# Four score tiles of each head group maximised over an fp16 copy made by ScalarE, with a new attention order and three reordered norm stages

## The chip, the cores and the metric

The kernel runs on one core of one Trainium2 chip. The metric is the device time in microseconds. Engines are TensorE (PE in the profile), its weight loads (PEld), VectorE (DVE), ScalarE (ACT), GpSimd (POOL) and SyncE, which issues the DMAs (SPq).

## The reference

Two layers over 1024 tokens of width 512, each half of a layer followed by a residual and a layer norm:

```python
x = layernorm(x + selective_scan(x))          # 16 states, softplus dt
x = layernorm(x + (silu(x @ Wg.T) * (x @ Wu.T)) @ Wd.T)          # 1792 wide
x = layernorm(x + attention(x))               # 32 heads of 16, rope, causal softmax, wo
x = layernorm(x + ffn(x))                     # 1376 wide, 4-bit GPTQ weights
```

The softmax of head n and token t is over `scores[n, t, s] / 4` for s <= t. Any number near the row's maximum may be subtracted before the exponential; the kernel searches that maximum first.

## The kernel before

Everything lies in one SBUF arena; each engine has one hand-written program, and semaphores order them.

*Scan* (to 201 us): 64 scans of VectorE (line 1354), products by GpSimd, sums by TensorE. *First norm*: `turn_first`, `first_stats`, `first_shift`, `first_normalise`, `turn_normed`, and `first_high` and `first_rest`, which split a normalised tile into two fp16 parts; `xl_done` counts tiles whose remainder is there. *First FFN* (213 to 363 us): 28 units `gate_up0(n)` (line 603), each of half the tokens, 16 gate and 16 up matmuls of 512 columns. `unit0_slot` gives unit n its two PSUM banks: units 0 to 3 alternate between two slots, unit 4 has the slot of unit 2 and waits for its Silu (`silu_done`). Then `down0` and the projections of q, k and v tile by tile (line 710), with rope on VectorE, the split by ScalarE and GpSimd, and the transposes `turn_stack`.

*Attention.* Heads go in NG = 8 groups of four (two pairs r, and two row halves b = 0, 1 of the array, 64 rows each). Search units (`search`, line 694; `max_units`): the scores of one query tile i against up to 512 keys, query on the PSUM rows, of one head, or of two heads where the columns are few: 40 units a group, 12 for the first four tiles (half 0) and 28 for the others (half 1). The last key tile of a row gets a mask added by two small matmuls (line 706). VectorE reduces each unit to its negated maximum (`maxima`, line 1563). `negate` (line 1581) joins the two key ranges of half 1, `turn_maxima` (line 733) transposes the maxima to rows, `keep_rows` (line 1587) copies them, and `put_rows` on SyncE sends them into q_st, where they are an additional row of the queries. So `keys` (line 743) gives scores with the maximum already subtracted, in the layout key by query; ScalarE takes the exponential (line 1114), GpSimd zeroes the corner of diagonal tiles (line 1254), `values` (line 757) multiplies with v and a column of ones, using the whole array in four column tiles. `keep_out` (line 1100), `turn_out` and `divide` finish a half of a group.

Search units, turns and outputs share a ring of three PSUM banks (`ring_slot`, line 684): unit n waits until unit n - 3 is read (`ring_read`). Keys have two pairs of banks, values one bank. The order of all steps, the same for all engines, is `ORDER`: the letters of `PATTERN` (s search, k keys, v values, n negate, t turn, o out) are gone through once for each group, and `START` says at which step of its own sequence each letter begins. 24 of group 0's search units (tiles below 6) are done early, during the projections (`early_units`, at most two at each of three places in a tile's projections), in a ring of two banks in which unit n waits for n - 1 reads.

*Second norm* (664 to 702 us): `second_out` (the wo projection), `second_stats`, `second_shift`, `second_root`, `second_normalise`, `second_turn`, `second_high`, `second_low`; then `gate_up1` of the second FFN, which wants four remainders (`xl_done`) for its first half of tokens and all eight for the second. *Second FFN* to 811 us, unpacking the 4-bit weights on VectorE, GpSimd and ScalarE beside it, and `down1` with the last norm (`norm_stage(3, ..., turn=False)`), each tile written out as it is done.

## Time and profile before

| | us |
|---|---|
| median of 3 runs | 879.1 (876.25 to 879.51) |
| profiled execution | 876.1 |
| its span | 874.4 |
| TensorE busy | 804.1 (92%) |
| VectorE busy | 642.1 (73%) |
| ScalarE busy | 443.5 (51%) |
| GpSimd busy | 301.8 (35%) |

The span is from the first to the last instruction. A busy share is that of the whole span, over stages with different limits. A matmul's row reaches to its modelled end, so rows of matmuls that follow each other overlap, and TensorE can read as busy where its array isn't full. A row of the order of time joins neighbours of one kind (xN), and "[... <-X]" is idle time before it and what ended it.

### The profile page before, as it was taken

How to read it: one execution, taken by the hardware profiler on the slowest of the kernel's cores; microseconds unless marked ns; L12 is line 12 of the kernel's file. 1: busy time of each engine (PE TensorE's matmuls, PEld its weight loads, DVE VectorE, ACT ScalarE, POOL GpSimd, SP SyncE). 2: the span in 40 equal slices, each digit the busy share in tenths (PEclk: the TensorE clock that was granted, in tenths of full speed). 3: DMA queues.
4: the chain of work that ended last, by engine and by line, in shares of the span. 5: the costliest groups of instructions: out<-in, count | busy, mean ns of one | idle time of the engine just before them, and what ended most of it. 6: DMA issues, size and time to landing. Idle time of an engine off the chain costs nothing.

```text
span 874.4 us, 19489 instructions
## 1 busy us (share of the span) xinstructions
PE 804.1 (92%) x8137; PEld 383.5 (44%) x8137; DVE 642.1 (73%) x900; ACT 443.5 (51%) x584; POOL 301.8 (35%) x217
## 2 busy tenths in 40 slices
PE   7669787787999999999989999999989999999997
PEld 2434344444444444455544444444424444444443
DVE  4999999997565333444669999999976677775344
ACT  4976666546654321254427777777786433332100
POOL 0699899991001000155421222121143222221000
PEclk9589999999999999999988999999999999999999
DMA  6900000005230000000000000000132013330001
GB/s 215 365 3 3 3 3 2 3 4 168 97 115 1 1 0 1 1 1 1 1 1 2 2 2 2 2 2 3 37 115 86 1 59 118 123 110 0 13 36 48
DMA packets 20017, 38.25 MB, mean 44 GB/s; under 512 B 5009, under 2 KB 10961, under 8 KB 19938
## 3 DMA queue, kind: packets, MB, share of 16 engines
q1 hardware_dynamic: 19938, 37.10, 12.4%
q8 instruction: 61, 1.00, 0.5%
q14 instruction: 18, 0.15, 0.1%
HBM read 34.87 MB, written 2.16 MB: 42 GB/s over the span
## 4 chain that ended last, share of the span: by engine, by line
PE 76%; DVE 13%; issue 4%; POOL 3%; ACT 2%; DMA 1%; SPq 1%; DVEq 0%; ACTq 0%; POOLq 0%
PE ps L832 13%; PE ps L613 11%; PE ps L590 10%; PE ps L769 8%; DVE arena L1354 7%; PE ps L702 7%; PE ps L867 7%; PE ps L666 6%; PE ps L753 3%; PE ps L706 3%; POOL arena L1205 2%; PE ps L679 2%; PE ps L509 2%; PE ps L465 1%; PE ps L778 1%
## 5 line engine op out<-in xcount | busy, mean ns | idle before, releaser
L1563 DVE TENSOR_REDUCE arena<-ps 128x1 f16<-128x512 f32 (+3 forms) x320 | 181.4, 630 | 6.4 <-PE ps L706 4.1
L1114 ACT ACTIVATE arena<-ps 128x1024 f32<-128x1024 f32 (+2 forms) x160 | 143.4, 940 | 60.6 <-PE ps L753 58.8
L1205 POOL TENSOR_TENSOR arena<-arena 128x1024 f32<-128x1024 f32 x62 | 152.0, 2485 | 9.3 <-DVE arena L1354 8.9
L1354 DVE TENSOR_TENSOR_SCAN arena<-arena,ps 128x1024 f32<-128x1024 f32 x64 | 142.1, 2269 | 2.0 <-PE ps L509 1.7
L832 PE MATMUL ps<-arena 128*128 128x512 f16 x528 | 114.5, 379 | 1.4 <-DVE arena L1671 1.4
L702 PE MATMUL ps<-arena 64*128 64x512 f16 (+3 forms) x384 | 99.6, 339 | 0.7
L1254 POOL TENSOR_SCALAR_AFFINE_SELECT arena<-arena 128x512 f32<-128x512 f32 x64 | 43.4, 685 | 162.4 <-ACT arena L1114 162.3
L613 PE MATMUL ps<-arena 128*128 128x512 f16 x448 | 97.5, 379 | 1.5 <-DVE arena L1494 1.5
L957 ACT ACTIVATE arena<-arena,negA 128x1024 f32<-128x1024 f32 x64 | 72.8, 1146 | 45.4 <-DVE arena L1354 43.2
L509 PE MATMUL ps<-arena 64*128 64x64 f16 x3072 | 60.0, 196 | 35.1 <-DVE arena L1354 31.8
L509 PEld LDWEIGHTS ps<-arena 64*128 64x128 f16 x3072 | 52.2, 98 | 86.3 <-DVE arena L1354 75.0
L590 PE MATMUL ps<-arena 128*128 128x512 f16 x384 | 86.6, 379 | 1.6 <-DVE arena L1453 1.6
L769 PE MATMUL ps<-arena 128*32 128x512 f32 (+3 forms) x768 | 80.2, 497 | 0.3 <-POOL arena L1254 0.3
L832 PEld LDWEIGHTS ps<-arena 128*128 128x128 f16 x528 | 51.6, 98 | 63.3 <-DVE arena L1671 1.6
L465 PE MATMUL ps<-arena,ident_sb 64*64 64x512 f32 x512 | 71.5, 634 | 2.0 <-POOL arena L1205 1.2
L753 PE MATMUL ps<-arena 64*128 64x512 f16 (+3 forms) x384 | 70.3, 328 | 2.4 <-ACT arena L1114 2.2
L613 PEld LDWEIGHTS ps<-arena 128*128 128x128 f16 x448 | 43.7, 98 | 53.6 <-issue 1.7
L702 PEld LDWEIGHTS ps<-arena 64*128 64x128 f16 x384 | 30.8, 94 | 69.0 <-DVE arena L1563 49.6
L867 PE MATMUL ps<-arena 128*128 128x512 f16 x264 | 57.1, 379 | 0.0
L706 PE MATMUL ps<-mask_b,picks_b 64*128 64x128 bf16 x512 | 55.9, 221 | 0.0
L590 PEld LDWEIGHTS ps<-arena 128*128 128x128 f16 x384 | 36.4, 98 | 43.7 <-DVE arena L1453 1.8
L666 PE MATMUL ps<-arena 128*128 128x512 f16 x224 | 49.3, 379 | 0.0
(173 smaller groups left out, 973.1 us busy)
## 6 DMA issues: line engine op xcount, KB each, us to landing
arena<-in_w_q_dram SPq DMA_DIRECT2D x11, 768.0 KB, 4.2
arena<-c_rows SPq DMA_DIRECT2D x16, 512.0 KB, 10.7
arena<-in_w_s_dram SPq DMA_DIRECT2D x11, 384.0 KB, 4.9
arena<-in_x_fm_dram SPq DMA_DIRECT2D x8, 256.0 KB, 4.3
out_dram<-arena SPq DMA_DIRECT2D x8, 256.0 KB, 2.0
arena<-in_wg_dram SPq DMA_DIRECT2D x1, 1792.0 KB, 10.2
arena<-in_wu_dram SPq DMA_DIRECT2D x1, 1792.0 KB, 7.3
arena<-in_wd_dram SPq DMA_DIRECT2D x1, 1792.0 KB, 11.3
```

The costliest lines, as they stand in the source:

```text
L509: last = nc.tensor.matmul(ps[:, 2 * (i % 2) + r, q * SUB:(q + 1) * SUB], dtx_tok[c % 2][rows, s, q, :], diag[n][rows, e, q, :], start=(k = ...
L590: last = nc.tensor.matmul(banks(bank, 1), part[:, c, ds(t * P, P)], wsp[:, w, s, c, :], start=(c == 0 and part is src_h and s == 0), stop= ...
L613: last = nc.tensor.matmul(banks(bank, 1), w[:, c, m * P:(m + 1) * P], part[:, c, h * HALF:(h + 1) * HALF], start=(c == 0 and part is xh), ...
L666: last = nc.tensor.matmul(banks(u, 1), part[:, m, ds(t * P, P)], wd0_sb[:, m, :], start=(m == 0 and part is hh), stop=(m == M0 - 1 and par ...
L702: last = nc.tensor.matmul(dst, q_st[rows, 2 * g + r, i * P:(i + 1) * P], k_st[rows, 2 * g + r, key:key + w], start=True, stop=not diag)
L769: last = nc.tensor.matmul(ps[32 * a:32 * a + 32, 7, lo - HALF * half:HALF], v_ring[g % 2][:, j, a, :], p_t[n % 4][:, a, 0:hi - lo], start= ...
L832: last = nc.tensor.matmul(banks(bank + h, 1), gu[u][:, s, w * DC + c, :], part[:, c, h * HALF:(h + 1) * HALF], start=(c == 0 and s == 0 an ...
L867: last = nc.tensor.matmul(banks(u, 1), part[:, m, ds(t * P, P)], wd1[:, s, m, :], start=(m == 0 and part is h1h and s == 0), stop=(m == M1 ...
L1114: nc.scalar.activation(dst, src, ACT.Exp, scale=float(HD) ** -0.5).then_inc(exp_done, 1)
L1205: nc.gpsimd.tensor_tensor(hC[i % 4][:], hst[i % 3][:], c_all[:, n, :], ALU.mult).then_inc(hc_done, 1)
L1354: nc.vector.tensor_tensor_scan(hst[i % 3][:], dA[i % 3][:], banks(2 * (i % 2), 2), 0.0, ALU.mult, ALU.add).then_inc(scan_done, 1)
L1563: nc.vector.reduce_max(maxima_slot(half, k), ps[:, ring_bank(n), 0:len(heads) * w].rearrange("p (a w) -> p a w", a=len(heads)), AX, negate ...
```

## The change

1. `SEARCH` is put in a new order of units, and `PATTERN` and `START` are others. The counts of each letter are the same (40 s, 20 k, 12 v, two each of n, t, o).
2. Four search units a group (`by_scalar`: half 1, keys 0 to 511, head r = 0, b = 0 of each of the four tiles; in group 0 only those of tiles 6 and 7) are no longer reduced from PSUM by VectorE. ScalarE copies them as fp16 to `s_copy`, which frees the ring bank (`ring_copied`); VectorE folds all four at once: three pair maxima and one reduction, put into its program behind the third later search unit or right before the join (`FOLD_AT`).
3. The turn of group 0's first half becomes early unit 14, in the projections of tile 6.
4. `gate_up0(0)` is done in two halves of columns, the first behind two remainders.
5. Second norm: ScalarE's `second_high` comes before the next root, VectorE's `second_low(t - 2)` before `second_shift(t)`, and the first `gate_up1` pieces are interleaved otherwise with the turns.
6. The last tile of `down1` is done in two halves of 256 columns in two banks, and its norm in halves too.

```diff
+        UNIT_ORDER = ((1, 8, 3, 5, 0, 4, 11, 2, 10, 7, 6, 9),
+                      (10, 8, 12, 25, 27, 5, 18, 21, 0, 4, 19, 11, 26, 13, 20, 15, 2, 9, 23, 14, 3, 24, 1, 22, 7, 6, 17, 16))
+        SEARCH = [[max_units(half)[k] for k in UNIT_ORDER[half]] for half in range(2)]
...
+        EARLY_TURN = len(max_units(0)) + 2
+        EARLY_UNITS.insert(EARLY_TURN, None)
...
+            return ([EARLY_TURN] if (t, place) == (6, 1) else []) + units[2 * place:2 * place + 2]
...
-        PATTERN = ("sskkssvvnssskktossvsksksssksksnvsskvsks"
-                   "vssksktosksvskssksvskkssvssksvssskvsskv")
-        START = {'s': 36, 'k': 0, 't': 1, 'o': -1, 'v': -2, 'n': 1}
+        PATTERN = ("ssvsskovssktskssvsskokssvkssvkskssvkssk"
+                   "vssksnkvskssvkktsvssksssvssskkssnvssksk")
+        START = {'k': 10, 'v': 2, 's': 57, 'n': 3, 't': 2, 'o': -1}
...
+        def by_scalar(g, half, k):
+            i, key, _, heads = SEARCH[half][k]
+            return half == 1 and key == 0 and heads == ((0, 0),) and (g > 0 or i >= EARLY_TILES)
...
+        def read_to(n):
+            return n + 1 - COPIED_TO[n]
...
+            pe.wait_ge(xl_done, TT // 4)
+            gate_up0(0, 0, HALF // 2)
             pe.wait_ge(xl_done, TT // 2)
-            gate_up0(0)
+            gate_up0(0, HALF // 2, HALF)
...
                 elif n >= EARLY + RING:
-                    pe.wait_ge(ring_read, n - RING + 1)
+                    if COPIED[n - RING - EARLY]:
+                        pe.wait_ge(ring_copied, COPIED_TO[n - RING])
+                    else:
+                        pe.wait_ge(ring_read, read_to(n - RING))
...
             second_turn(4)
-            second_turn(5)
             pe.wait_ge(w1_low, 1)
             pe.wait_ge(xl_done, 2 * TT + TT // 2)
             gate_up1(0, 0, (0,), first=True, only=(0,))
+            second_turn(5)
             second_turn(6)
             pe.wait_ge(ln_taken, TT + 7)
-            gate_up1(0, 0, (0,), first=True, only=(1,))
+            gate_up1(0, 0, (0,), first=True, only=(1,), chunks=(0, 1))
             second_turn(7)
+            gate_up1(0, 0, (0,), first=True, only=(1,), chunks=(2, 3))
...
+            def copy_scores(g, half, k, n):
+                act.wait_ge(ring_full, n + 1)
+                if g:
+                    act.wait_ge(folded, g)
+                nc.scalar.copy(s_copy[:, SEARCH[half][k][0] - 4, :], ps[:, ring_bank(n), :]).then_inc(ring_copied, 1)
...
             for t in range(TT - 2):
+                second_high(t)
                 if t + 3 < TT:
                     second_root(t + 3)
                 second_normalise(t + 2)
-                second_high(t)
...
+                def take_last(src_bank, lo, hi):
+                    dve.wait_ge(x_kept, TT * ln)
+                    src = xtok[:, TT - 1, lo:hi]
+                    own.done(nc.vector.tensor_scalar(o_half[:, lo:hi], banks(src_bank, 1)[:, lo:hi], scale, None, ALU.mult))
+                    own.done(nc.vector.tensor_tensor(src, src, o_half[:, lo:hi], ALU.add))
+                    at = 6 * lo // (hi - lo)
+                    own.done(nc.vector.bn_stats(st12[:, at:at + 6], src))
...
+            def fold_scores(g):
+                some = slice(first_copied(g), 4)
+                dve.wait_ge(ring_copied, copied_before(g + 1))
+                nc.vector.tensor_tensor(s_copy[:, some, 0:256], s_copy[:, some, 0:256], s_copy[:, some, 256:512], ALU.max).then_inc(halved, 1)
+                dve.wait_ge(halved, 2 * g + 1)
+                nc.vector.tensor_tensor(s_copy[:, some, 0:128], s_copy[:, some, 0:128], s_copy[:, some, 128:256], ALU.max).then_inc(halved, 1)
+                dve.wait_ge(halved, 2 * g + 2)
+                nc.vector.tensor_tensor(s_fold[:, some, :], s_copy[:, some, 0:64], s_copy[:, some, 64:128], ALU.max).then_inc(folded, 1)
+                dve.wait_ge(folded, g + 1)
+                nc.vector.reduce_max(m_neg[1][:, some, 0], s_fold[:, some, :], AX, negate=True).then_inc(m_folded, 1)
...
             second_stats(0)
             second_stats(1)
-            for t in range(TT):
+            second_shift(0)
+            second_stats(2)
+            second_shift(1)
+            for t in range(2, TT - 1):
+                second_stats(t + 1)
+                second_low(t - 2)
                 second_shift(t)
-                if t + 2 < TT:
-                    second_stats(t + 2)
-                if t >= 2:
-                    second_low(t - 2)
+            second_shift(TT - 1)
+            second_low(TT - 3)
```

The first unpacking of 4-bit weights on VectorE moves from behind an output of group 6 to behind the last turn of group 7.

## Rows read from the trace of the kernel before

**Rows 1.** Order of time, VectorE: start us, us, engine line op out<-in xcount.
```profile
539.89 0.42 DVE L1581 TENSOR_TENSOR arena<-arena 128x16 f16<-128x16 f16 x1
...
550.66 0.68 DVE L1563 TENSOR_REDUCE arena<-ps 128x1 f16<-128x512 f32 x1
551.26 0.40 DVE L1587 COPY arena<-ps 4x512 f16<-4x512 f16 x1
...
565.51 0.42 DVE L1581 TENSOR_TENSOR arena<-arena 128x16 f16<-128x16 f16 x1
```
**Rows 2.** Stretches: length, busy PE, PEld, DVE, ACT, POOL, PEclk, DMA share, GB/s.
```profile
539.90:565.50 25.60, 25.52 (x274) 11.33 (x272) 24.85 (x47) 18.79 (x23) 5.57 (x10) 1.00 0.01 2
642.40:664.30 21.90, 17.13 (x154) 5.24 (x153) 13.78 (x20) 17.98 (x22) 13.84 (x10) 1.00 0.24 78
```
**Rows 3.** Groups by shape, 488 to 642: xcount | busy us, mean ns | idle before.
```profile
L702 PEld LDWEIGHTS ps<-arena 64*128 64x128 f16 x288 | 23.3, 93 | 53.9 <-DVE arena L1563 39.7 <-DVE arena L1594 5.0 <-issue 3.7
...
L1100 ACT COPY arena<-ps 128x512 f32<-128x512 f32 x13 | 7.6, 588 | 0.0
```
**Rows 4.** Order of time, TensorE, one values step and its successors.
```profile
552.11 1.07 PE L769 MATMUL ps<-arena 128*32 128x512 f32 x8
553.11 0.39 PE L702 MATMUL ps<-arena 64*128 64x512 f16 x1
553.11 0.39 PE L753 MATMUL ps<-arena 64*128 64x512 f16 x1
```
**Rows 5.** Order of time, first FFN, units 2 and 4.
```profile
229.08 0.60 ACT L1032 ACTIVATE arena<-ps 128x512 f32<-128x512 f32 x1
...
229.74 4.49 PE L613 MATMUL ps<-arena 128*128 128x512 f16 x20
```
**Rows 6.** Order of time, projections of tile 6.
```profile
432.10 0.69 DVE L1552 TENSOR_TENSOR arena<-ps,cos_sb 128x512 f32<-128x512 f32 x1 [1.36 <-PE ps L590]
...
432.88 0.39 PE L702 MATMUL ps<-arena 64*128 64x512 f16 x2
...
433.21 2.76 PE L590 MATMUL ps<-arena 128*128 128x512 f16 x12
433.37 1.21 DVE L1558 COPY arena<-ps 128x2048 f16<-128x2048 f16 x1
```
**Rows 7.** Order of time, start of attention: first turn, first join.
```profile
453.28 0.38 PE L740 MATMUL ps<-ident_h,arena 128*4 128x128 f16 x4 [1.47 <-issue]
...
463.44 0.17 DVE L1581 TENSOR_TENSOR arena<-arena 128x16 f16<-128x16 f16 x1
```
**Rows 8.** Order of time, VectorE operations on pairs, and GpSimd beside the last.
```profile
198.72 1.22 DVE L1370 TENSOR_TENSOR arena<-arena 128x1024 f32<-128x1024 f32 x1 [0.20 <-DVE arena L1370]
...
551.97 0.42 DVE L1594 TENSOR_TENSOR arena<-ps,arena 128x256 f32<-128x256 f32 x1
...
707.52 3.11 POOL L1272 TENSOR_TENSOR arena<-arena 128x1536 f32<-128x1536 f32 x1 [9.55 <-DVE arena L1609]
...
709.80 1.90 DVE L1690 TENSOR_TENSOR arena<-arena 128x1024 f16<-128x1024 f32 x1 [1.11 <-ACT arena L1173]
```
**Rows 9.** Order of time, ScalarE behind the last join.
```profile
645.27 5.43 ACT L1114 ACTIVATE arena<-ps 128x1024 f32<-128x1024 f32 x6 [1.27 <-PE ps L753]
```
**Rows 10.** Order of time, TensorE, second norm to second FFN.
```profile
691.18 0.60 PE L820 MATMUL ps<-ident_sb,arena 128*128 128x128 f32 x4
...
693.89 0.63 PE L820 MATMUL ps<-ident_sb,arena 128*128 128x128 f32 x4 [2.11 <-DVE arena L1671]
...
694.35 2.75 PE L832 MATMUL ps<-arena 128*128 128x512 f16 x12
...
701.97 14.20 PE L832 MATMUL ps<-arena 128*128 128x512 f16 x65 [1.40 <-DVE arena L1671]
```
**Rows 11.** Order of time, VectorE, last tile.
```profile
867.95 0.69 DVE L1423 TENSOR_SCALAR arena<-ps 128x512 f16<-128x512 f32 x1 [3.98 <-PE ps L867]
...
871.33 0.55 DVE L1449 TENSOR_SCALAR arena<-arena,mv,rstd 128x512 f32<-128x512 f32 x1
```

More of the change, by code:

```diff
@@ L256, in attention_order @@
                         continue
+                    if (kind, g, half) == ("turn", 0, 0):
+                        continue
                     order.append((kind, g, half, *rest))
@@ L1121, in _ @@
                     keep_out(g, half)
+                elif kind == "search" and by_scalar(g, half, *at):
+                    copy_scores(g, half, *at, RING_AT[kind, g, half, *at])
             def high_out(t):
@@ L1587, in keep_rows, with early, negate @@
                 nc.vector.tensor_copy(m_row[0:GH, half * HALF:(half + 1) * HALF], ps[0:GH, ring_bank(n), :].bitcast(f16)[:, 0:HALF]).then_inc(ring_read, 1)
+            def early(n):
+                if n == EARLY_TURN:
+                    keep_rows(0, 0, n)
+                else:
+                    maxima(*EARLY_UNITS[n], n)
+            for t in range(TT):
+                rope(0, t)
+                for n in early_units(t, 0):
+                    early(n)
+                rope(1, t)
+                if t:
+                    keep_keys(t - 1)
+                for n in early_units(t, 1) + early_units(t, 2):
+                    early(n)
+            keep_keys(TT - 1)
+            def fold_scores(g):
[8 more added lines that the diff above has]
+                nc.vector.reduce_max(m_neg[1][:, some, 0], s_fold[:, some, :], AX, negate=True).then_inc(m_folded, 1)
+            FOLD_AT = {}
+            for g in range(NG):
+                at_last = max(n for n, step in enumerate(ORDER) if step[0] == "search" and step[1] == g and by_scalar(*step[1:]))
+                later = [n for n, step in enumerate(ORDER) if n > at_last and (step[0] == "search" or step == ("negate", g, 1))]
+                join = ORDER.index(("negate", g, 1))
+                FOLD_AT[min(later[2], join)] = g
+            def negate(g, half):
+                if half:
+                    dve.wait_ge(m_folded, g + 1)
+                    dve.wait_ge(ring_read, searched(g, 1))
+                    nc.vector.tensor_tensor(m_neg[1][:], m_neg[1][:], m_b[:], ALU.min).then_inc(m_joined, 1)
             def divide(g, half, n):
@@ L1623, in weights_low @@
                 dve.wait_ge(w1_low, m + 1)
-            for kind, g, half, *at in ORDER:
+            for n, (kind, g, half, *at) in enumerate(ORDER):
+                if n in FOLD_AT:
+                    fold_scores(FOLD_AT[n])
+                if kind == "search" and by_scalar(g, half, *at):
+                    continue
                 if kind == "search":
@@ L1638, in _ @@
                         unscaled(0)
-                    elif g == NG - 1 and half == 0:
+                elif kind == "out":
+                    divide(g, half, RING_AT[kind, g, half])
+                    if g == NG - 1 and half == 0:
                         first_weights_high()
```

112 lines of the change are left out of this document (66 added, 46 removed).

## The prediction

> **What bounds the kernel now.** I read the busy times by stretch first, then the order of time of the stretches that the edits touch, then the groups by shape, each time asking which wait ends last.
>
> Attention is most of it. Its inner part repeats exactly: the join of the second half's maxima on VectorE (line 1581) comes at 539.89 and again at 565.51, so one head group takes 25.62 us [rows 1]. In that period VectorE is busy 24.85 us, TensorE 25.52, ScalarE 18.79, GpSimd 5.57 [rows 2]. VectorE is the pace: its 40 row maxima of a group come 0.60 us apart when nothing holds them (550.66 to 551.26) [rows 1], and TensorE's weight loads for search units stood 39.7 us of six periods behind line 1563, mostly while an earlier matmul still ran [rows 3]. But TensorE is hardly behind. A values step holds the whole array for 1.00 us (552.11 to 553.11), while a search and a keys matmul start together because they use different halves of the rows [rows 4]. I count the streams of one group: search and keys 18432 columns each, the masks 8192; two of them side by side at best. At 0.216 us per 512 columns (65 of them in 14.20 us [rows 10]) that is 19.0 us one after the other and 9.5 us perfectly paired. The values steps take 10 us (six of 1.00, and twice 0.8, 0.6 and 0.4 for the shorter ones, by their columns: 9.6, and the changes between whole array and halves), the turns some 2 us. 25.6 us leaves 13.6 us for the 19.0 us of half-array work, so most of what can be paired is paired. That is how a busy of 25.52 has to be read: not proof of a full array, but near to it.
>
> **The change part by part.**
>
> *First norm (half of unit 0's columns before the rest).* TensorE could start unit 0 about 1.5 us sooner. Unit 4 needs the Silu of unit 2 (same banks). That Silu ran at 229.08 for 0.60 us, and unit 4's stream started at 229.74, 0.06 us after its end [rows 5]. ScalarE's chain of table loads, roots and normalising before that Silu isn't changed. The gain turns into a wait there: 0 (bounds -0.1 and +0.1).
>
> *Early turn.* The turn of group 0's maxima goes into the projection of tile 6, as ring unit 14, ahead of two search units. A ring unit n waits for n - 1 reads, so the second of them waits until VectorE has read the turn. VectorE gets there behind the rope of k and keep_keys(5), which began at 433.37 and took 1.21 us; then 0.40 us for the rows: 434.9. TensorE stands before that unit from about 433.3, then streams it 0.25 us, so the v projection starts at 435.2 instead of 433.21 [rows 6, 1]. This stretch is TensorE's own chain: +1.9 us (0 if VectorE were ready, +2.2 at most). Queued behind the waiting unit are the v projection and all of tile 7.
>
> *Start of attention.* Turn to first join took 453.28 to 463.44 [rows 7]. Gone: the turn and its row copy ahead of the search (0.3 us) and two of 16 maxima (1.2 us); added a fold of two tiles (about 1.3 us by the prices below): -0.2 us. The rows' transfer no longer stands before group 0's keys, but in the new order 15 search units do, so the keys hardly come sooner.
>
> *A full period, VectorE.* Four of 40 maxima go: 4 x 0.60 = 2.40 us. Added are three maxima of fp16 pairs of 1024, 512 and 256 elements a partition and a reduction of 256, each waiting for the one before. No row of before has an fp16 pair operation of such size. As fp32 does it: 1.22 us for 1024 and 0.42 for 256 [rows 8], 0.69 for 512 [rows 6], 0.42 for the last, with waits 2.8 us: +0.4 us a group. At two elements a cycle, as the fp16 copy of 2048 elements out of PSUM does in 1.21 us [rows 6]: 0.69 + 0.42 + 0.29 + 0.42 and the waits, 1.87 us: -0.53 us. I take the faster, since that copy has the same types. One more price: where GpSimd multiplied (707.52 to 710.63), VectorE's pair operation of 1024 took 1.90 us rather than 1.22 [rows 8]. GpSimd is busy 5.57 us in 25.6, so a fold meets it about one time in five: +0.1 us.
>
> The Trainium skill (VectorE: DVE Perf Modes, "The perf-mode tier table") gives tensor_tensor twice the rate for 16-bit operands in SBUF and tensor_reduce none; by it the fold costs 1.9 us rather than 2.8. SBUF — State Buffer, "Who interferes with whom", has a two-input VectorE operation and a GpSimd one lock each other out for whole instructions. The 1.90 us row agrees with that, and it speaks against the fold.
>
> *A full period, the others.* ScalarE gets four copies of 0.59 us [rows 3]: 18.79 + 2.36 = 21.2 of 25.6 us. Behind a copy stand the exponentials; behind its ring slot stands the third next search unit. TensorE has the same streams in another order. Counted in the code, the whole-array steps of a group fell into 13 runs and now into 15; a change in and back costs 0.1 us each way, so +0.4 us. Neighbouring units on opposite row halves stay 15 of the search pairs, and three pairs are now both on half 0. So VectorE offers up to 0.5 us and TensorE, which has little of its own to give, takes most of it back. I take -0.15 us a period (bounds -0.53 and +0.40): 7 x -0.15 = -1.05 us, ends -3.7 and +2.8.
>
> *End of attention.* From the last join to the output turns it took 642.4 to 664.3, ScalarE busy 17.98 of 21.9 [rows 2], exponentials 0.91 us apart [rows 9]. The new order leaves one keys unit more and three values steps more (0.8, 0.6, 0.4 us) and a ScalarE copy behind the last join: 0.9 + 0.6 us on ScalarE, 2.0 on TensorE, partly side by side: +1.6 us (0 to +2.3).
>
> *Second norm.* TensorE stood 2.11 us before the turn of tile 5 and 1.40 us before the rest of the first up and gate units [rows 10]. Now VectorE's remainder comes ahead of the shift and ScalarE's high part ahead of the next root, so the four remainders that the gate unit needs end at about 690.7 instead of 693.7. TensorE's work from the end of turn 4 (691.18, and 0.45 to the next operation) is three turns at 0.46 and 24 matmuls at 0.216: 698.2 at the soonest. Followed step by step, tile 6 is normalised at 694.9, tile 7 at 696.3, the last remainder ends at 698.55, and TensorE goes on at 698.65 instead of 701.97: -3.3 us (-2.5 to -3.6). What follows is TensorE without a gap, and the weight chain moves with it.
>
> *Last tile.* From TensorE's end to the last normalised row took 867.95 to 871.88, three passes of 0.69 among it [rows 11]. Half of each is done beside the second half's matmuls, and tile 6's reciprocal and normalising leave the chain: 0.42 x 3, 0.19, 0.29, 0.17, 0.55 and waits make 2.7 us: -1.25 us.
>
> Sum: 0 + 1.9 - 0.2 - 1.05 + 1.6 - 3.3 - 1.25 = -2.3 us. The profiled execution took 876.1 us with a span of 874.4, near the lowest run (876.25) and 3.0 under the median (879.1). It would become 873.8, and the median 876.8 us.
>
> **The rivals.**
> 1. *VectorE's relief comes through whole* (for it: 39.7 us of waits; against it: TensorE's 25.52). 7 x -0.53 instead of -1.05 is 2.65 us less: 874.1 us.
> 2. *The slot held by ScalarE.* A copy stands behind queued exponentials. With two ahead it frees its slot after 2 x 1.02 + 0.59 = 2.6 us, where three maxima take 1.8, so TensorE and then VectorE stand 0.8 us. If this costs 0.4 us for each of the 30 copies: +12 us, 888.8 us, slower than before. It decides from the point where a second exponential is in front. Against it: ScalarE idles 6.8 us a period, and a values step lies before each copied unit.
> 3. *The fold at one element a cycle*: periods +0.4 instead of -0.15, 880.6 us. A mild loss or nothing.
> 4. *The second norm doesn't do what it says*, since the remainders still come last: +3.3 us, 880.1 us.
>
> **How the numbers follow.** Forecast 0.50, rivals 0.25, 0.08, 0.10, 0.07. About 0.5% (4.4 us) is what a measurement of this kernel can tell from no change: faster lies under 874.7, slower over 883.5. Half of rival 1 and a fifth of the forecast, with its own bounds of some 2 us and the runs' 3 us between them, lie under 874.7: 0.28. Slower is rival 2 and a little of 3: 0.10. Range: down past rival 1 with the last bounds, 872.0, up past rivals 3 and 4, 882.0.
>
> **What would show it.** Joins 25.3 to 25.6 us apart; about 25.1 is rival 1; over 25.9 rival 2 or 3. Pair maxima of 1024 elements at 0.69 us or 1.22 us. Weight loads of search units waiting for the new ScalarE copy for over 0.5 us a group would be rival 2. A gap of near 2 us in TensorE in tile 6 of the projections. TensorE's gap before unit 4 of the first FFN instead of before unit 0. TensorE restarting the second FFN 3.3 us nearer to the end of attention. The prediction is wrong above all if pairing on the array improves with the new order more than my count of neighbours shows.

## The result

The changed kernel takes 879.5 us (median of 20 runs, 876.5 to 881.7) beside 876.2 us for the kernel before on the same chip (20 runs, 874.0 to 879.5): ratio 1.0025, 95% interval 1.0013 to 1.0037. It is slower by 0.25%. I had forecast 2.3 us less; it took more: 2.2 us by the ratio, 3.3 us between the two medians.

**The profile after.** The first lines of the page:

```profile
span 879.2 us, 19568 instructions
...
PE 810.3 (92%) x8186; PEld 392.5 (45%) x8186; DVE 638.7 (73%) x905; ACT 457.9 (52%) x614; POOL 302.4 (34%) x217
```

VectorE lost 3.4 us, ScalarE gained 14.4, and the span went from 874.4 to 879.2. Busy times don't say where. I took the order of time of both traces, looked up the start of the same step in each, and subtracted from one step to the next:

| from ... to | before | after | change | forecast |
|---|---|---|---|---|
| start ... end of scan (code unchanged) | 197.21 | 198.19 | +0.98 | 0 |
| ... first transposes of the projections | 179.40 | 179.55 | +0.15 | 0 |
| ... last k transposes | 74.98 | 78.07 | +3.09 | +1.9 |
| ... first join (group 0) | 11.85 | 12.20 | +0.35 | -0.2 |
| ... second join, first period | 25.20 | 26.62 | +1.42 | -0.15 |
| ... eighth join, six periods | 153.75 | 153.61 | -0.14 | -0.9 |
| ... first output turn | 21.91 | 23.65 | +1.74 | +1.6 |
| ... turn of tile 0 in the second norm | 14.77 | 16.32 | +1.55 | 0 |
| ... 25th operation of the first up and gate units | 22.90 | 19.62 | -3.28 | -3.3 |
| ... end | 172.41 | 171.41 | -1.00 | -1.25 |

The mark of the last k transposes is the start of the last of them. The seven periods that I had priced together at -1.05 us took 1.28 us more, nearly all of it in the first.

The scan isn't touched, and ended between 195.3 and 198.9 us in the traces of the runs below, so they are compared from step to step and not by their spans.

*Periods.* Order of time, VectorE: two joins (line 1692, in the kernel before line 1581) and the fold ahead of the second. Then the stretch between them (columns as in [rows 2]), and two groups of weight loads by shape, 494 to 648 us (columns as in [rows 3]).

```profile
545.84 0.19 DVE L1692 TENSOR_TENSOR arena<-arena 128x16 f16<-128x16 f16 x1
...
569.48 0.68 DVE L1673 TENSOR_TENSOR arena<-arena 128x1024 f16<-128x1024 f16 x1
570.19 0.42 DVE L1675 TENSOR_TENSOR arena<-arena 128x512 f16<-128x512 f16 x1
570.65 0.29 DVE L1677 TENSOR_TENSOR arena<-arena 128x256 f16<-128x256 f16 x1
570.98 0.42 DVE L1679 TENSOR_REDUCE arena<-arena 128x4 f16<-128x256 f16 x1
571.43 0.19 DVE L1692 TENSOR_TENSOR arena<-arena 128x16 f16<-128x16 f16 x1
```
```profile
545.90:571.50 25.60, 25.42 (x278) 11.31 (x274) 24.34 (x48) 20.64 (x27) 5.58 (x10) 1.00 0.01 2
```
```profile
L748 PEld LDWEIGHTS ps<-arena 64*128 64x128 f16 x283 | 22.0, 93 | 34.5 <-DVE arena L1642 28.5 <-issue 4.3
L802 PEld LDWEIGHTS ps<-arena 64*128 64x128 f16 x290 | 17.9, 94 | 21.2 <-ACT arena L1170 16.4 <-issue 3.5
```

VectorE is busy 24.34 instead of 24.85 us [rows 2], the 0.5 us that I had worked out, and the joins are 25.59 us apart instead of 25.62 [rows 1]. The waits for the maxima (line 1642) fell from 39.7 us [rows 3] to 28.5, and 16.4 us of waits for exponentials (line 1170) stand ahead of the keys' weight loads, where the kernel before waits 2.5 us in all (line 753, 488 to 642 us).

*Projections.* Order of time, the turn of group 0 in tile 6 (lines 762 and 748; VectorE lines 1637, 1649).

```profile
434.14 0.39 PE L762 MATMUL ps<-ident_h,arena 128*4 128x128 f16 x4
...
434.62 1.22 DVE L1637 COPY arena<-ps 128x2048 f16<-128x2048 f16 x1
...
435.75 0.40 DVE L1649 COPY arena<-ps 4x512 f16<-4x512 f16 x1
...
436.30 0.37 PE L748 MATMUL ps<-arena 64*128 64x512 f16 x1 [1.34 <-DVE arena L1649]
...
436.61 2.76 PE L630 MATMUL ps<-arena 128*128 128x512 f16 x12
```

That is the gap I described, in its place: 1.34 us, where I had said near 2.

*End of attention.* Order of time, TensorE, VectorE and GpSimd.

```profile
665.14 3.54 POOL L1312 TENSOR_SCALAR_AFFINE_SELECT arena<-arena 128x512 f32<-128x512 f32 x2 [0.40 <-ACT arena L1170]
...
666.11 2.07 DVE L1714 SCALAR_TENSOR_TENSOR arena<-arena 128x1536 f32<-128x1536 int32 x1
...
668.82 0.43 PE L818 MATMUL ps<-arena 128*32 128x128 f32 x8 [1.47 <-POOL arena L1312]
...
671.89 6.12 PE L853 MATMUL ps<-ident_sb,arena 128*128 128x128 f32 x32 [0.88 <-DVE arena L1699]
```

Two corner masks took 3.54 us beside a pair operation of VectorE, and TensorE waited for them. The output turns (line 853) then ran at half clock (1.2 GHz). Stretches, columns as in [rows 2], of the changed kernel and then of the kernel before, whose output turns began at 664.30 us:

```profile
672.00:676.00 4.00, 4.00 (x20) 4.00 (x20) 2.01 (x3) 2.15 (x4) 0.00 (x0) 0.50 0.60 217
```
```profile
664.00:668.00 4.00, 3.54 (x27) 2.95 (x28) 2.56 (x5) 2.93 (x7) 0.56 (x1) 1.00 0.55 183
```

*Second norm.* Order of time, TensorE, after [rows 10]: the gaps of 2.11 and 1.40 us there are gone.

```profile
700.75 2.75 PE L881 MATMUL ps<-arena 128*128 128x512 f16 x12
703.34 1.36 PE L869 MATMUL ps<-ident_sb,arena 128*128 128x128 f32 x8
704.53 1.46 PE L881 MATMUL ps<-arena 128*128 128x512 f16 x6
705.83 0.60 PE L869 MATMUL ps<-ident_sb,arena 128*128 128x128 f32 x4
706.26 3.90 PE L881 MATMUL ps<-arena 128*128 128x512 f16 x16
```

### The profile page after: what moved, and what is told of

The parts are those of the page before. It is cut to its first block, busy times and chain, and to the rows that moved or that the text cites. A ratio compares the mean times of both kernels' runs of the same rounds, so it can differ in the third digit from the quotient of the medians.

```text
span 879.2 us, 19568 instructions
## 1 busy us (share of the span) xinstructions
PE 810.3 (92%) x8186; PEld 392.5 (45%) x8186; DVE 638.7 (73%) x905; ACT 457.9 (52%) x614; POOL 302.4 (34%) x217
## 4 chain that ended last, share of the span: by engine, by line
PE 71%; DVE 16%; issue 5%; ACT 4%; POOL 3%; DMA 1%; SPq 1%; DVEq 0%; POOLq 0%; ACTq 0%
PE ps L881 13%; PE ps L630 10%; PE ps L653 9%; DVE arena L1412 7%; PE ps L818 7%; PE ps L917 6%; PE ps L709 5%; PE ps L748 5%; PE ps L802 3%; PE ps L752 2%; POOL arena L1263 2%; DVE arena L1642 2%; PE ps L722 2%; PE ps L500 2%; PE ps L544 1%
## 5 line engine op out<-in xcount | busy, mean ns | idle before, releaser
L1642 DVE TENSOR_REDUCE arena<-ps 128x1 f16<-128x512 f32 (+3 forms) x290 | 166.5, 627 | 12.0 <-PE ps L752 5.0
L881 PE MATMUL ps<-arena 128*128 128x512 f16 x528 | 114.6, 379 | 0.1
L653 PE MATMUL ps<-arena 128*128 128x512 f16 (+1 forms) x464 | 97.6, 372 | 1.0 <-ACT arena L1082 1.0
L748 PE MATMUL ps<-arena 64*128 64x512 f16 (+3 forms) x384 | 93.0, 340 | 4.9 <-DVE arena L1637 1.5
L544 PE MATMUL ps<-arena 64*128 64x64 f16 x3072 | 61.2, 197 | 33.0 <-DVE arena L1412 29.3
L630 PE MATMUL ps<-arena 128*128 128x512 f16 x384 | 86.6, 379 | 1.6 <-DVE arena L1511 1.6
L802 PE MATMUL ps<-arena 64*128 64x512 f16 (+3 forms) x384 | 68.7, 333 | 1.6 <-ACT arena L1170 1.3
L752 PE MATMUL ps<-mask_b,picks_b 64*128 64x128 bf16 x512 | 58.8, 222 | 0.0
L917 PE MATMUL ps<-arena 128*128 128x512 f16 (+1 forms) x297 | 57.2, 355 | 0.0
L1272 POOL COPY arena<-arena 128x512 f32 x24 | 14.7, 613 | 101.2 <-DVE arena L1507 46.1
```

The costliest lines, as they stand in the source:

```text
L544: last = nc.tensor.matmul(ps[:, 2 * (i % 2) + r, q * SUB:(q + 1) * SUB], dtx_tok[c % 2][rows, s, q, :], diag[n][rows, e, q, :], start=(k = ...
L630: last = nc.tensor.matmul(banks(bank, 1), part[:, c, ds(t * P, P)], wsp[:, w, s, c, :], start=(c == 0 and part is src_h and s == 0), stop= ...
L653: last = nc.tensor.matmul(banks(bank, 1)[:, lo:hi], w[:, c, m * P:(m + 1) * P], part[:, c, h * HALF + lo:h * HALF + hi], start=(c == 0 and ...
L748: last = nc.tensor.matmul(dst, q_st[rows, 2 * g + r, i * P:(i + 1) * P], k_st[rows, 2 * g + r, key:key + w], start=True, stop=not diag)
L802: last = nc.tensor.matmul(ps[:, 3 + 2 * (e % 2) + b, at * (hi - lo):(at + 1) * (hi - lo)], k_st[rows, 2 * g + r, j * P:(j + 1) * P], q_st[ ...
L881: last = nc.tensor.matmul(banks(bank + h, 1), gu[u][:, s, w * DC + c, :], part[:, c, h * HALF:(h + 1) * HALF], start=(c == 0 and s == 0 an ...
```

## The experiments

Joins are given as the distance from the second to the eighth in the run's trace, divided by six; within a trace single distances agree to 0.03 us where nothing else is said.

**1. The parts put together otherwise.** Four kernels, 6 or 12 timed executions each, beside the kernel before (877.99 us, 23 executions).

`norms_only`: the kernel before with edits 4, 5 and 6 alone.

```diff
-            return half == 1 and key == 0 and heads == ((0, 0),) and (g > 0 or i >= EARLY_TILES)
+            return False
```
(PATTERN, START, the order of units and the place of the turn are also as before, and the fold is left out.)

> The kernel before with the edits of the three norms and the last tile alone (no ScalarE copies, order and turn as before). Theory (the norms give what was forecast, the rest of the change takes it back): the second norm gives -3.3 us, the last tile -1.1, the first norm 0, so 871.7 us against 876.1, ratio 0.995. Rival (the norms gain nothing once attention isn't late, for the second FFN then waits for its weights): ratio 0.999 to 1.000.

871.25 us (869.8 to 874.3), ratio 0.992 (0.989 to 0.995): faster than the kernel before and, by the two ratios, than the changed kernel. Joins 25.63 us. In its trace the second norm gave 3.27 us and the last tile about 1.1, as expected. The median moved 6.7 us where these terms make 4.4, the lower end of what its interval allows (4.3 to 9.8); what the rest is stays open. In its trace the operations from the eighth join to the second norm took 0.8 us more than before, at a granted clock of 0.86 and 0.71 (660 to 668 us).

`copy_old_order`: that kernel with copies and fold, in the old order of attention.

> As the changed kernel, but with the pattern, the unit order and the late turn of the kernel before: the ScalarE copies and folds are in. Theory (TensorE is near its own limit, so VectorE's relief of half a microsecond a group comes through only in part): joins 25.3 to 25.6 us apart, total 870 to 871.7 us. Rival 1 (the relief comes through whole in the old order): joins 25.1 us apart, 868 us. Rival 2 (the slot held by ScalarE stalls TensorE): joins over 25.9 us apart, over 873.5 us.

897.0 us (893.1 to 898.5), ratio 1.021 (1.018 to 1.024). Joins are 27.91 us apart, and 29.2 or 29.3 twice, in stretches where the granted clock was 0.96 and 0.95. This is rival 2, in the prediction as in this expectation. Who waited for the copies, 468 to 650 us, first in this kernel, then in the changed one, where the list is empty:

```profile
L1148 ACT CAST arena<-ps x26: 586/589/622, 473.5 to 647.3; 128x512 f16<-128x512 f32 x26
...
who waited for it (us, times):
  PEld ps L740: 6.6, 13
  PE ps L740: 2.9, 7
```
```profile
L1156 ACT CAST arena<-ps x28: 586/586/587, 477.4 to 645.3; 128x512 f16<-128x512 f32 x28
```

Most copies follow other work of ScalarE without a pause in both (20 of 26, and 21 of 28: the list of idle times has 6 and 7). The difference is that here somebody wants the slot meanwhile: over some seven periods weight loads of search units waited 6.6 us for it, nearly 1 us a group. The two rows can't be added, since a weight load waits beside matmuls that still run; and the seven periods lost 20.7 us, so these waits alone don't account for it. In the period from the join at 550.90 VectorE idled 3.3 us, where it idled 0.75 before:

```profile
550.90:578.81 27.91, 25.58 (x274) 10.83 (x274) 24.59 (x47) 20.61 (x27) 5.91 (x9) 0.99 0.01 2
```

`turn_none`: the changed kernel with the turn of group 0 left in attention.

```diff
-        EARLY_UNITS.insert(EARLY_TURN, None)
+        EARLY_TURN = None
```
(and what places the turn is as before)

> The changed kernel with the turn of group 0 left in the attention order. Theory (the early turn is worth nothing, since 15 search units stand before group 0's first keys anyway): 2 us less than the changed kernel, 877 us, first exponential less than 1 us later relative to the last keys copy. Rival (the row transfer of over 2 us would stand before the keys): as slow as the changed kernel or slower, 879.5 us and more.

876.85 us (873.6 to 883.0), ratio 0.999 (0.9965 to 1.001). From the first to the last transposes of the projections 75.88 us: 2.19 less than the changed kernel, and 0.90 more than before. The 0.90 us come from the new order of units, 24 of which lie in the projections: all four kernels with new units and no early turn start these transposes 75.03 us behind the first ones, and the six with the old units and the same masks and waits 74.13 or 74.14. The early turn costs the rest. Of the 2.19 us, 0.38 are the transposes themselves, 16 of which took 1.54 us at half clock in the changed kernel's trace and 1.07 here; counted to the start of the first of them the turn costs 1.81 us. From there to the second join it takes 38.70 us, 0.12 less than with the early turn: the turn gives nothing back. The first exponential came 11.8 us behind the last k transposes instead of 11.2, so the theory holds in that too.

`turn_16`: the turn after both search units of its place, not ahead of them.

```diff
-        EARLY_TURN = len(max_units(0)) + 2
+        EARLY_TURN = len(max_units(0)) + 4
```

> The changed kernel with the early turn two ring units later (unit 16, behind both search units of its place), so that TensorE has a projection to do before it needs the turn read. Theory (the early turn costs 2.2 us of TensorE standing in tile 6): -2.0 to -2.5 us against the changed kernel, 877 us, and the gap of 1.34 us before a search unit is gone. Rival (the stall only moves to a later tile): within 0.5 us of the changed kernel.

879.35 us, ratio 1.0005 (0.998 to 1.003), projections 79.40 us, 1.3 more than in the changed kernel (1.7 to the first of the last transposes). The wait is not gone, it stands before the turn:

```profile
434.42 0.38 PE L762 MATMUL ps<-ident_h,arena 128*4 128x128 f16 x4 [1.45 <-DVE arena L1642]
434.73 4.45 PE L630 MATMUL ps<-arena 128*128 128x512 f16 x12
```

Twelve matmuls behind it took 4.45 instead of 2.76 us, at a granted clock of 0.65 (434 to 438 us). My theory falls, and the rival is right. The maxima that the turn transposes (tiles 0 to 3) had been read long before. What it waits for is a bank: in the ring of two a unit waits until the last but one ahead of it is read. That was the search unit that VectorE reached at 433.85, behind the rope and keep_keys (line 1637), so a third step of the ring in this place has the wait wherever it stands.

**2. What paces a period.** One timed execution each, with its trace. The first takes 1.0 us a group off VectorE: the fold's three steps and its reduction over 8 columns, so the four maxima are not found.

```diff
-                nc.vector.tensor_tensor(s_copy[:, some, 0:256], s_copy[:, some, 0:256], s_copy[:, some, 256:512], ALU.max)
+                nc.vector.tensor_tensor(s_copy[:, some, 0:8], s_copy[:, some, 0:8], s_copy[:, some, 256:264], ALU.max)
```

> The changed kernel with the fold cut to 8 columns a tile at each of its steps, so its maxima are over fewer scores: VectorE is relieved of a further 1 us or so a group. Theory (TensorE sets the period of the changed kernel): joins stay 25.5 to 25.6 us apart. Rival (VectorE still sets it): joins 24.6 to 24.9 us apart.

Joins 25.29 us: a third of what was taken off VectorE comes through, between theory and rival. The next two leave out one of the two mask matmuls of each diagonal piece, 32 matmuls of 128 columns a group, in the changed kernel and in the kernel before.

```diff
-                        for s in range(2):
+                        for s in range(1):
```

> The changed kernel with one of the two mask matmuls of a diagonal score tile left out (half of the masking of the search is missing): TensorE has 4096 columns less a group, 1.7 us one after the other and about 0.9 us where two run side by side. Theory (TensorE sets the period of the changed kernel): joins 0.5 to 1.2 us closer, 24.4 to 25.1. Rival (VectorE sets it): 25.6 still.

> The kernel before with one of the two mask matmuls of a diagonal score tile left out (half of the masking of the search is missing). Theory (there VectorE sets the period, TensorE a little behind): joins 25.2 to 25.6 us apart, at most 0.4 less than 25.62. Rival (TensorE set it there already): 0.5 to 1.2 us less.

Joins 25.24 us (-0.36) in the changed kernel, which neither theory nor rival had, and 25.35 us (-0.28) in the kernel before, as expected. 32 masks are about 1.7 us of streaming at 0.054 us each, so a sixth to a fifth of that comes through. My theory for the changed kernel, that TensorE had become the pace, falls too. Relief of either engine comes through in part, so I read the period of both kernels as a chain that goes back and forth between the engines; I didn't follow it link by link.

**3. Copies and order, one at a time.** The same norms and last tile, no early turn; order of units, order of steps and copies changed singly. One timed execution each.

`new_no_copy`:

```diff
-            return half == 1 and key == 0 and heads == ((0, 0),) and (g > 0 or i >= EARLY_TILES)
+            return False
```

> The changed kernel without the ScalarE copies and without the fold, and with the turn of group 0 left in attention: VectorE takes all 40 maxima of a group, in the new order. Its partner is the earlier run with the turn left in attention and the copies kept (joins 25.60 us apart). Theory: both engines carry the pace a little. The light fold gave back 0.35 us a group for 1.0 us taken off VectorE; here VectorE gets 4 x 0.60 = 2.40 us and loses 1.87 us of fold, so joins 25.7 to 25.9 us apart, and the copies are worth about 0.2 us a group in the new order. Rival 1: TensorE alone sets 25.60: joins within 0.05 us of it, and copies and fold are worth nothing. Rival 2: the new order stands on the copies: joins over 26.1 us.

`units_new_only`, and `units_new_copy` with copies, go back to the old steps:

```diff
-        PATTERN = ("ssvsskovssktskssvsskokssvkssvkskssvssk"
-                   "vssksnkvskssvkktvsssksssvssskkssnvssksk")
-        START = {'k': 10, 'v': 2, 's': 57, 'n': 3, 't': 2, 'o': -1}
+        PATTERN = ("sskkssvvnssskktossvsksksssksksnsvsskvsks"
+                   "vssksktosksvskssksvskkssvssksvssskvsskv")
+        START = {'s': 36, 'k': 0, 't': 1, 'o': -1, 'v': -2, 'n': 1}
```

> The norms and the last tile as changed, no copies, the turn in attention, the old order of steps, the new order of units. Old order of both: joins 25.62 us apart; new order of both: 26.44. Theory: the order of the units costs, since two neighbours on the same half of the array can't run side by side: joins 26.0 to 26.4 us. Rival: it is the order of the steps: joins 25.6 to 25.8 us.

`steps_new_only`, and `steps_new_copy` with copies, go back to the old units:

```diff
-        SEARCH = [[max_units(half)[k] for k in UNIT_ORDER[half]] for half in range(2)]
+        SEARCH = [max_units(half) for half in range(2)]
```

> The norms and the last tile as changed, no copies, the turn in attention, the new order of steps, the old order of units. Theory (units): joins 25.6 to 25.9 us. Rival (the steps cost, with two more changes between whole array and halves and search units in threes): 26.2 us or more.

> As the run with the new order of units alone, with copies and fold. Old order of both with copies: 28.5 us between joins (25.6 without); new order of both with copies: 25.60. Theory: the place of the copied units among the steps decides, and the old steps send copies in behind queued exponentials whatever the units: joins over 27 us. Rival: the new order of units alone spreads the copied units enough: under 26 us.

> As the run with the new order of steps alone, with copies and fold. Theory: the new steps give the copies room in ScalarE's queue: joins 25.2 to 25.9 us. Rival: the copied units stand together in the old order of units, and joins are over 26.5 us.

| us between joins | no copies | copies and fold |
|---|---|---|
| old units, old steps | 25.63 (`norms_only`) | 28.35 (`copy_old_order`) |
| new units, old steps | 26.50 (`units_new_only`) | 30.02 (`units_new_copy`) |
| old units, new steps | 27.75 (`steps_new_only`) | 29.66 (`steps_new_copy`) |
| new units, new steps | 26.44 (`new_no_copy`) | 25.60 (`turn_none`) |

In `units_new_copy` single distances lie between 28.9 and 30.4 us, the shortest where the granted clock was 1.00 and the others where it was 0.94; all the others but `copy_old_order` are steady.

This settles where the relief of VectorE went. The new order by itself costs 0.81 us a group; the copies in it give back 0.84, more than the 0.5 us by which VectorE's busy time falls. Both halves of the order cost when they come alone, the steps more (2.1 us), and neither makes the copies bearable: only the two together do. That the units alone carry the cost, and that the steps alone give the copies room, were both wrong. The period of `new_no_copy`:

```profile
546.45:572.85 26.40, 26.23 (x276) 11.40 (x273) 24.91 (x47) 18.73 (x23) 5.60 (x9) 1.00 0.01 2
```

VectorE is as busy as before, 24.91 us, and idles 1.5 us of it instead of 0.75: the order, not an engine's load, made it longer. Its keys' weight loads wait for exponentials, 9.2 us from 546 to 643 us, where the kernel before has 0.2 us of it in about as long a stretch (548 to 643 us):

```profile
L796 PEld LDWEIGHTS ps<-arena 64*128 64x128 f16 x172 | 11.0, 93 | 10.3 <-ACT arena L1164 9.2 <-issue 0.5
```

```profile
L753 PEld LDWEIGHTS ps<-arena 64*128 64x128 f16 x178 | 11.0, 94 | 1.8 <-ACT arena L1114 0.2 <-issue 0.2
```

These waits come with the new steps, but they aren't what the 0.81 us is made of. The changed kernel has the same 9.2 us of them in 548 to 643 us at 25.60 us a period, and `units_new_only`, as slow as `new_no_copy`, has 0.8 us (546 to 643 us):

```profile
L796 PEld LDWEIGHTS ps<-arena 64*128 64x128 f16 x178 | 12.7, 94 | 1.5 <-ACT arena L1164 0.8
```

Which neighbours in the order make a period longer stays open.

`old_light_copy` asks what holds the slot in the old order: each copy cut to 8 of 512 columns (the four maxima are not found).

> The run with copies and fold in the old order (joins 25.9 to 29.3 us apart, 27.6 in the mean of the last seven... 28.0 at most), with each ScalarE copy cut to 8 of 512 columns, so that the maxima of the four units are not found. The copy still waits behind what is queued on ScalarE and frees the slot at its end. Theory: the place in ScalarE's queue holds the slot, not the 0.59 us of the copy: joins still over 27.0 us apart in the mean. Rival: the copies' own time is what ScalarE and the slots lack: joins 25.6 to 26.5 us.

Joins 27.45 us in the last four periods, where the full copies had 27.91 and 29.30 (the first three were 28.6 to 31.5, in stretches with a granted clock of 0.91, 0.91 and 0.87). So the copy's own time is 0.46 us of the 2.3 that the old order loses at the least. The rest doesn't hang on how long a copy takes. I put it down to the copy's place in ScalarE's queue; the place of the fold in VectorE's program would show in the same way, and no run parts the two. (The means over six periods, 28.35 us in both, can't be compared: the stretches at a lower clock aren't the same.)

**4. The end of attention.** `small_unscaled` does the pair operation of VectorE beside the last masks (line 1714) over 8 columns for that one weight tile, whose values are then wrong.

> The changed kernel with VectorE's unscaled(1) over 8 of its 1536 columns (one tile of the second FFN's weights is left out). Theory (that operation, with both inputs in SBUF, holds GpSimd's last corner masks at the end of attention, and the idle TensorE then falls to half its clock for the output turns): the two masks at 665 us take 1.3 instead of 3.5 us, output turns start 2 us sooner and take 4 us at the full clock instead of 6, together -3 us. Rival (the masks are slow for another reason): no change of the masks, and at most -0.3 us.

Order of time, GpSimd; then TensorE:

```profile
662.06 2.02 POOL L1312 TENSOR_SCALAR_AFFINE_SELECT arena<-arena 128x512 f32<-128x512 f32 x2 [0.40 <-ACT arena L1170]
```
```profile
666.88 5.38 PE L853 MATMUL ps<-ident_sb,arena 128*128 128x128 f32 x24 [0.88 <-DVE arena L1699]
```

The masks fell from 3.54 to 2.02 us, and the eighth join to the first output turn from 23.65 to 21.73 us, less than in the kernel before. So the collision of the two is shown, and it is all of this stretch's +1.7 us. The masks didn't fall to the 1.3 us expected. The output turns still ran long, at a granted clock of 0.50 and 0.88 (668 to 676 us), and to the second norm 1.4 of the 1.9 us are left. Of the 3 us expected half came.

**5. The clock at the start of attention.** Stretches of the changed kernel (columns as in [rows 2]; the third from the end is the granted clock).

```profile
456.00:460.00 4.00, 2.45 (x14) 1.06 (x13) 2.72 (x4) 0.59 (x1) 0.00 (x0) 0.50 0.00 0
460.00:464.00 4.00, 3.89 (x14) 1.21 (x13) 3.90 (x8) 0.59 (x1) 0.00 (x0) 0.50 0.00 0
464.00:468.00 4.00, 2.81 (x20) 1.54 (x17) 3.81 (x9) 0.98 (x2) 0.00 (x0) 0.50 0.00 0
468.00:472.00 4.00, 3.95 (x37) 2.40 (x37) 2.69 (x7) 3.39 (x5) 1.67 (x3) 0.50 0.00 0
```

TensorE stood 1.96 and 1.52 us around the last k transposes and then had half the clock (1.2 GHz) up to 472 us, 4.0 us behind the first join; the kernel before had it to 464 us only, 0.5 us behind its first join:

```profile
460.00:464.00 4.00, 4.00 (x33) 2.79 (x32) 3.94 (x9) 1.94 (x2) 0.35 (x1) 0.51 0.00 0
464.00:468.00 4.00, 3.95 (x49) 1.97 (x46) 3.55 (x8) 2.36 (x3) 0.92 (x2) 1.00 0.00 1
```

The first period follows it. With order, copies and fold of the changed kernel it took 25.94 us where the full clock was back 1.5 us behind the first join (`turn_none`), 26.05 at 1.9 us (`turn_16`), 26.51 at 3.1 us (`small_unscaled`) and 26.62 at 4.0 us (the changed kernel). So about half of its +1.42 us goes with the clock. `fill_new` (the changed kernel) and `fill_norms` (the kernel of `norms_only`) put transposes into the two waits, whose results are overwritten: 24 and 20 of them.

```diff
             pe.wait_ge(q_kept, TT)
+            for _ in range(24):
+                nc.tensor.transpose(turned[:, 0:P], tok_stack[:, 0, 0:2, :].rearrange("p h d -> p (h d)"), ident_h[:])
             turn_stack(1, TT - 1)
```

> The changed kernel with 24 transposes, whose result is overwritten, put into TensorE's wait before the last transposes of k, and 20 more into its wait for keep_keys before the first search unit of attention. Theory: the clock fell to half there (456 to 472 us in the changed kernel) because TensorE had stood 1.96 and 1.52 us; with the waits filled it stays at 1.00 for all or most of 456 to 472, the last transposes take 1.06 instead of 1.54 us, and the second join (after group 1) comes 1.0 to 1.8 us sooner, measured from the last k transposes. Rival: TensorE's thin search work behind the wait makes it fall all the same, some us later; then the second join moves by less than 0.5 us.

> The kernel before with the changed norms and last tile alone (measured 871.25 us, ratio 0.992), with the same filling transposes. Theory: the clock stays at 1.00 at the start of attention, but here the old order loses nothing to it (the second join came 35.4 us behind the turn with it at half for 10 us, and joins follow each other 25.2 us apart there): within 0.5 us of the norms alone, so 870.7 to 871.7 us, ratio 0.991 to 0.993. Rival: the search units at half clock (0.64 us against VectorE's 0.60) hold VectorE here too: 1.0 us or more less, under 870.3 us.

The first 24 stood behind the wait that they should fill, and came on top of it: in `fill_new` the last k transposes were 2.5 us later, and the second join, counted from the first of them, 1.2 us sooner, as expected, but later in all; `fill_norms` took 875.9 us (872.9 to 880.2; ratio 0.998, 0.996 to 1.001) instead of the 870.7 to 871.7 expected. In its trace 1.3 us of that lie before the last k transposes and 0.8 us between them and the second join. So neither says much; `fill_in_gap` has the 24 ahead of that wait, in the bank of the first search unit.

> The changed kernel, its two waits at the start of attention filled with 24 and 20 transposes that go to a bank that the first search unit overwrites; the first 24 are now ahead of the wait for ScalarE's copy of q. Theory: the last k transposes aren't later than in the changed kernel, the clock is at 1.00 up to 458 us or beyond, and the second join comes 1.0 to 2.0 us sooner, counted from the first v projection (116.9 us in the changed kernel). Rival: the clock falls in 451 to 456 all the same, and the second join moves less than 0.5 us.

(The mark that it calls the first v projection is the first transposes of the projections.) The clock stayed at 1.00 up to 460 us, and then fell all the same:

```profile
456.00:460.00 4.00, 3.17 (x19) 1.30 (x19) 3.31 (x6) 0.60 (x2) 0.00 (x0) 1.00 0.00 0
460.00:464.00 4.00, 2.46 (x9) 0.59 (x10) 3.80 (x10) 0.57 (x1) 0.00 (x0) 0.53 0.00 0
464.00:468.00 4.00, 3.95 (x31) 2.48 (x33) 3.15 (x7) 2.69 (x4) 0.63 (x1) 0.50 0.00 0
```

The second join came 0.8 us sooner (116.1 instead of 116.9), between the two expectations, and all of it ahead of the first join. With the clock up, a search unit is done sooner and TensorE stands between units until VectorE has read one: 3.17 and 2.46 of 4 us busy, and the clock fell again, until 470.4 us. So the two waits aren't the only cause. That the other is the search stretch, in which VectorE paces a TensorE that has nothing else, is my reading; no run fills that stretch.

## Why the prediction was wrong, point by point

- *First norm*, 0: measured +0.15. TensorE started unit 0 1.5 us sooner and stood 0.98 us for the Silu (line 1082), as forecast.
- *Early turn*, +1.9: measured +1.8 to the start of the transposes behind it, 2.2 with their half clock, by the run that takes it out. Right. What I left out is that a new order of units also moves those that lie in the projections: +0.9 us.
- *Start of attention*, -0.2: measured +0.35 to the first join, and the first period, which I had at -0.15 as one of seven, measured +1.42. I priced maxima against the fold and took the rest as it was. From the last k transposes to the second join `norms_only` takes 37.13 us and `turn_none` 38.70, so the new order and the copies cost 1.6 us here, with or without the early turn. The order alone is dearer still (40.37 us in `new_no_copy`, where the half clock lasted to 475 us). `light_fold` took 36.73 us, 2.1 less than the changed kernel; part of that may be the clock, which was back 2.5 us behind its first join instead of 4.0, so that the fold stands on the path here isn't shown by it alone.
- *Periods*, -1.05 for seven: measured +1.28, of it -0.14 in the last six. This is the largest miss. The price of the fold was right to 0.05 us (0.68, 0.42, 0.29, 0.42 measured), and with it the choice of the faster rate. The Trainium skill (VectorE: DVE Perf Modes, "The perf-mode tier table") agrees with these rows: the pair operations ran at twice the rate of fp32, and the reduction of 256 took the 0.42 us of an fp32 pair operation of 256. What failed is the price of the new order. TensorE takes the relief back, I had said, and offered 0.4 us for it, from a count of changes between the whole array and its halves, of which -0.15 us a period was to be left. The runs show 0.81 us for the order, 0.87 for the new units alone and 2.1 for the new steps alone. I had counted array time of one part and nothing for units and steps not fitting each other; what those microseconds are made of stays open. For the first period I had no term for the clock either.
- *End of attention*, +1.6: measured +1.74, but not by my count of work left over. Taking one VectorE operation away gave 1.9 us, more than the whole loss. The mechanism was in [rows 8], where I used it for the fold, and in a rule that I cited (Trainium skill, SBUF — State Buffer, "Who interferes with whom"): what moved next to the last masks was the unpacking, and they took 3.54 us beside it and 2.02 with it cut to 8 columns. In the period shown the fold's pair steps met no work of GpSimd (masks from 567.99 to 569.21 and from 570.97), and the 0.1 us I had charged for that wasn't due.
- *Behind it*, 0: measured +1.55. I had no term for it. The output turns ran at half clock from 672 to 676 us, where the kernel before ran its own at 1.00. Over all the traces this stretch took 14.8 us in six of the eight kernels with the old steps and 15.6 in the other two (`norms_only`, `fill_norms`), and 15.6 to 16.9 in all eleven with the new steps. So it comes with the new steps, at 1 to 2 us, though the 0.8 us of `norms_only`, whose waits are those of before, shows that single executions differ here too. That the longer waits ahead bring the lower clock fits the rows, and no run shows it.
- *Second norm*, -3.3, and *last tile*, -1.25: measured -3.28 and -3.27, and about -1.1, in the changed kernel and `norms_only`. (From the last matmul to the last normalised row it is 2.78 instead of 3.93 us; the table's -1.00 has the stretch ahead in it.) Followed step by step through rows of before, they came out as worked out. `norms_only` shows that they stand by themselves.
- *Rivals*. 2, the slot held by ScalarE, had 0.08. It didn't occur in the changed kernel, where nobody waited for a copy, but something like it happens in the old order, at 2.3 us a group and more: search units wait for the copy there. I had argued against it from ScalarE's idle 6.8 us a period, and that says little: copies stand in a queue in both orders, and the two lists of who waited differ in whether TensorE wants the slot meanwhile. 1, 3 and 4 didn't occur.

In sum, between the two traces, against the forecast: projections +1.2, up to the first join +0.55, the seven periods +2.3, the stretch behind the end +1.55 us, and 1.0 us of scan that is no effect of the change. The traces are 4.9 us apart and the kernels, by the ratio, 2.2: the scan, the clock at the start of attention and the clock behind its end are what single executions differ in.

Level and sign went apart: 879.5 us lies inside my range of 872.0 to 882.0, but that range stood around a median of three runs, 879.1, which 20 runs put at 876.2. That the figure fits is luck.

## What to carry to other kernels

Price a new order of steps as a change of its own, before what it is there to carry: here it took 0.81 us a group and the relief gave back 0.84, and each half of it alone made things worse. When a slot's reader is moved to another engine, ask when the slot is wanted next and what is queued there at that moment, not how idle the engine is on average. And where a change has parts that don't touch, time them apart: norms and last tile alone are 0.8% faster than the kernel before, which the whole hides.

## What the runs showed of the hardware

- A maximum of fp16 pairs out of memory took 0.68, 0.42 and 0.29 us for 1024, 512 and 256 elements a partition: 0.26 us for 512 elements, where the 1.22 and 0.42 us of 1024 and 256 fp32 elements [rows 8] make 0.53, and 0.16 us that doesn't shrink. The reduction of 256 fp16 elements took 0.42 us, as long as the fp16 pair step of 512.
- Two corner masks on GpSimd took 3.54 us beside VectorE's pair operation of 1536 from an int32 and an 8-bit input, and that took 2.07 us there and 1.76 at 711.53; with it cut to 8 columns they took 2.02. A mask alone took 0.63 to 0.80 us.
- A wait of TensorE of 1.45 us in tile 6 was followed by a granted clock of 0.65 (434 to 438 us) in `turn_16`, and one of 1.34 us by 1.00 (436 to 440 us) in the changed kernel. After the clock had been kept up by filling, it fell again over stretches in which TensorE was busy 3.17 and 2.46 of 4 us.
